# One layer of linear attention and a low-rank FFN: query-times-state product on sixteen 32x32 tiles in four banks, scores in the query's bank, four FFN value buffers

## The reference, cut to what matters

```python
xn = layernorm(x); x_norm = layernorm(xn) * ln_g + ln_b
q, k, v = split(x_norm @ W_qkv + b_qkv)
gate = sigmoid(xn @ W_gate + b_gate); gate = gate / (mean(gate) + EPS)
q = relu(q * gate) ** 2 + EPS;  k = relu(k * gate) ** 2 + EPS
# for each row t, by head:
kv = kv + k_t[:, None] * v_t[None, :];  ks = ks + k_t
out_t = (q_t @ kv) / (q_t . ks + EPS)
x1 = x + out @ W_proj + b_proj
# FFN, rank 128, hidden 2048:
y = x1 + gelu_tanh(layernorm(x1) @ U1 @ V1 + b1) @ U2 @ V2 + b2
```

## Time and profile before

| | |
|---|---|
| median of 3 runs | 1810.46 us (1809.34 to 1811.13) |
| profiled execution | 1809.73 us, span 1807.6 us |
| PE matmul busy | 1766.4 us, 98% |
| PE weight load busy | 1495.7 us, 83% |
| DVE busy | 1399.5 us, 77% |
| POOL busy | 822.7 us, 46% |
| ACT busy | 685.8 us, 38% |
| mean granted TensorE clock | 0.992 |
| DMA | 61.43 MB, mean 34 GB/s |

### The profile page before, as it was taken

One profiled execution on the slowest core, in us unless ns is written; L12 is line 12 of the kernel. 1 busy time (PEld: TensorE's weight loads), 2 busy tenths in 40 slices (PEclk: granted clock), 3 DMA queues, 4 the chain that ended last, 5 costly groups with the idle time before them and its releaser, 6 DMA issues. The chain is left out here.

```text
span 1807.6 us, 39914 instructions
## 1 busy us (share of the span) xinstructions
PE 1766.4 (98%) x16729; PEld 1495.7 (83%) x16729; DVE 1399.5 (77%) x2222; ACT 685.8 (38%) x1242; POOL 822.7 (46%) x1027
## 2 busy tenths in 40 slices
PE   7799999999999999999999999999999999999997
PEld 4688888888888888888888888888888888888876
DVE  6787787787787787777787777777777777777765
ACT  4233433433433433433433433433433433433332
POOL 3344544544544544544544544544454544454430
PEclk9899999999999999999999999999999999999999
DMA  6101010011010011010011011010100110100000
GB/s 206 34 19 36 25 36 25 24 37 36 25 36 25 25 37 33 28 36 25 25 36 29 32 29 27 30 36 25 36 25 29 32 37 24 37 24 26 30 19 24
DMA packets 34529, 61.43 MB, mean 34 GB/s; under 512 B 3672, under 2 KB 6256, under 8 KB 34352
## 3 DMA queue, kind: packets, MB, share of 16 engines
q1 hardware_dynamic: 33488, 57.31, 10.0%
q10 hardware_dynamic: 864, 1.57, 0.3%
HBM read 41.96 MB, written 16.91 MB: 33 GB/s over the span
## 5 line engine op out<-in xcount | busy, mean ns | idle before, releaser
L379 POOL TENSOR_TENSOR h_lo<-h_full,h_hi 128x512 fp32r<-128x512 f32 x244 | 313.5, 1285 | 483.5 <-DVE h_hi L605 483.5
L460 ACT ACTIVATE h_full<-ps_h,cols 128x256 f32<-128x256 f32 x512 | 211.1, 472 | 243.9 <-PE ps_h L783 236.4
L605 DVE CAST h_hi<-h_full 128x512 fp32r<-128x512 f32 x256 | 154.0, 602 | 98.2 <-ACT h_full L460 98.1
L781 PE MATMUL ps_b<-wx_hi,zt_hi 128*128 128x512 f32 x512 | 206.8, 404 | 5.0 <-DVE key_sums L711 3.1
L342 POOL TENSOR_TENSOR small<-moments,eps_col 128x1 f32<-128x1 f32 x128 | 25.7, 201 | 402.6 <-DVE moments L750 333.4
L781 PE MATMUL scores<-wx_hi,zt_hi 128*128 128x512 f32 x512 | 208.2, 407 | 0.0
L783 PE MATMUL ps_b<-wx_hi,zt_lo 128*128 128x512 f32 x512 | 204.1, 399 | 0.0
L782 PE MATMUL ps_b<-wx_lo,zt_hi 128*128 128x512 f32 x512 | 203.5, 397 | 0.0
L783 PE MATMUL scores<-wx_hi,zt_lo 128*128 128x512 f32 x512 | 202.1, 395 | 0.0
L782 PE MATMUL scores<-wx_lo,zt_hi 128*128 128x512 f32 x512 | 201.8, 394 | 0.0
L781 PE MATMUL ps_q<-h_hi,u_hi 128*128 128x256 f32 x512 | 154.1, 301 | 6.2 <-DVE h_lo L610 5.1
(11 more groups left out here) (156 smaller groups left out, 4498.6 us busy)
## 6 DMA issues: line engine op xcount, KB each, us to landing
xs<-L_attn_x SPq DMA_DIRECT2D x64, 256.0 KB, 2.7
out<-x1s SPq DMA_DIRECT2D x64, 256.0 KB, 2.1
key_sums<-carry_rows SPq DMA_DIRECT2D x60, 256.0 KB, 3.2
x1s<-L_attn_W_gate SPq DMA_DIRECT2D x4, 256.0 KB, 4.2
x1s<-L_ffn_U SPq DMA_DIRECT2D x4, 256.0 KB, 3.5
carry_rows<-key_sums SPq DMA_DIRECT2D x64, 2.0 KB
probs<-L_attn_W_qkv SPq DMA_DIRECT2D x3, 256.0 KB, 6.0
bias<-L_attn_b_qkv ACTq DMA_DIRECT2D x3, 256.0 KB, 6.8
```

The costliest lines, as they stand in the source:

```text
L379: E.tensor_tensor(h_lo[:, i % 2, :], h_full[:, i % 2, :], h_hi[:, i % 2, :].bitcast(F32), ALU.subtract).then_inc(s["h_lo_ready"], 1)
L460: last = E.activation(h_full[:, i % 2, a * GROUP:(a + 1) * GROUP], ps_h[i % 2][:, a * GROUP:(a + 1) * GROUP], ACT.Gelu_apprx_tanh, bias=b1 ...
L605: E.tensor_copy(h_hi[:, i % 2, :], h_full[:, i % 2, :]).then_inc(s["h_hi_ready"], 1)
L781: E.matmul(ps, wh, mh, start=start and i == 0, stop=False)
```

## The change

Six edits go together.

1. L944's products go to tiles (32j, 32ft), sixteen different tiles. Head group j writes bank `ps_out[j]`, partitions 32 ft. L986 accumulates there, on column tile ft. The output of a chunk now lies in 128 columns of each of four banks (`out_cols`), in another order of heads, so the rows of W_proj are loaded in that order, sixteen DMAs in place of four.
2. The product stands behind the masks: after scores, PE does `h_pair` 2, `h_pair` 3 and `q_pair` 0, then the product and L986, then tz, `q_pair` 1, L977, the sums, y, `q_pair` 2 and `q_pair` 3.
3. The eight banks are laid out anew. Scores take ps_t, ps_c, ps_d and ps_b, the query's bank, and no longer wait for `value_ready`; the product does, as ps_out is ps_c, ps_d, ps_b, ps_a.
4. `state` is double, so that the new state is written to the other half.
5. Four h buffers (`SLOTS`) in place of two.
6. ACT does gelu 2 and 3 ahead of `ot_hi`; POOL does `key_lo` ahead of the tail of pair 1; DVE takes probs ahead of the cast of pair 1, and `ot_lo` ahead of the state.

```diff
@@ -163,26 +163,33 @@
-        state = sb("state", [P, 4, KT, HEAD])
+        state = sb("state", [P, 2, 4, KT, HEAD])
         probs = sb("probs", [P, HPG, KT * P])
 ...
         qt_hi, qt_lo = pt_hi, pt_lo
-        h_hi = sb("h_hi", [P, 2, 2 * GROUP], F32R)
-        h_full, h_lo = sb_over("h_full", "h_lo", [P, 2, 2 * GROUP], F32R)
+        SLOTS = 4
+        h_hi = sb("h_hi", [P, SLOTS, 2 * GROUP], F32R)
+        h_full, h_lo = sb_over("h_full", "h_lo", [P, SLOTS, 2 * GROUP], F32R)
         lnb_wide = probs[:, 0, :].rearrange("p (k n) -> p k n", k=KT)
 ...
-        scores = ctx.enter_context(nc.psum_tensor("scores", [P, HPG * DM], F32))
-        ps_c, ps_d, ps_t, ps_a = (scores[:, j * DM:(j + 1) * DM] for j in range(HPG))
-        ps_b = bank("ps_b")
+        wide = ctx.enter_context(nc.psum_tensor("wide", [P, 5 * DM], F32))
+        ps_t, ps_c, ps_d, ps_b, ps_a = (wide[:, j * DM:(j + 1) * DM] for j in range(5))
+        scores = wide[:, 0:HPG * DM]
+        ps_scores = [ps_t, ps_c, ps_d, ps_b]
+        ps_out = [ps_c, ps_d, ps_b, ps_a]
+        out_cols = wide[:, DM:5 * DM].rearrange("p (j n) -> p j n", j=HPG)[:, :, 0:P]
         ps_h = [bank("ps_h0"), bank("ps_h1")]
         ps_q = bank("ps_q")
-        ps_scores = [ps_c, ps_d, ps_t, ps_a]
+
+        def state_of(c, turn=0):
+
+            return state[:, (c.p + c.off // 4 + turn) % 2, c.slot, :, :]
@@ -213,8 +220,8 @@
                        wx_lo[:, k, group, :], k, group) for k in range(KT)]
-        wp_v = w_proj.rearrange("(k p) n -> k p n", p=P)
-        tiles += [(wp_v[k, :, :], wp_hi[:, k, :], wp_lo[:, k, :], None, None) for k in range(KT)]
+        wp_v = w_proj.rearrange("(f j v) n -> j f v n", f=KT, j=HPG)
+        tiles += [(wp_v[k, :, :, :], wp_hi[:, k, :], wp_lo[:, k, :], None, None) for k in range(KT)]
         flat = "p k n -> p (k n)"
@@ -245,8 +252,11 @@
+        turned_tiles = range(FIRST, FIRST + KT)
+
         def tile_landed(eng, t):
-            eng.wait_ge(stage_in[stage_of(t)], 16 if t < FIRST else 16 * ((t - FIRST) // RING + 2))
+            here = [u for u in range(t + 1) if stage_of(u) == stage_of(t)]
+            eng.wait_ge(stage_in[stage_of(t)], sum(16 * KT if u in turned_tiles else 16 for u in here))
@@ -282,6 +292,11 @@
                             sp.wait_ge(s["stage_bias"], used)
+                    if t in turned_tiles:
+                        for f in range(KT):
+                            sp.dma_start(slot[f * HEAD:(f + 1) * HEAD, :], src[f, :, :])\
+                                .then_inc(stage_in[stage_of(t)], 16)
+                        continue
                     dst = slot if len(src.shape) == 2 else slot.rearrange("p (k n) -> p k n", k=src.shape[1])
@@ -376,7 +391,7 @@
                 pool.wait_ge(s["h_hi_ready"], g.done(PAIRS, i + 1))
-                E.tensor_tensor(h_lo[:, i % 2, :], h_full[:, i % 2, :], h_hi[:, i % 2, :].bitcast(F32),
+                E.tensor_tensor(h_lo[:, i % SLOTS, :], h_full[:, i % SLOTS, :], h_hi[:, i % SLOTS, :].bitcast(F32),
                                 ALU.subtract).then_inc(s["h_lo_ready"], 1)
@@ -399,12 +414,12 @@
                         h_tail(ffn, pairs[0])
-                    h_tail(ffn, pairs[1])
                 if n.exists:
 ...
                 if ffn.exists and not is_last(p):
+                    h_tail(ffn, pairs[1])
                     h_tail(ffn, pairs[2])
@@ -457,7 +472,7 @@
                 for a in range(2):
-                    last = E.activation(h_full[:, i % 2, a * GROUP:(a + 1) * GROUP],
+                    last = E.activation(h_full[:, i % SLOTS, a * GROUP:(a + 1) * GROUP],
                                         ps_h[i % 2][:, a * GROUP:(a + 1) * GROUP], ACT.Gelu_apprx_tanh,
@@ -499,13 +514,13 @@
                     gelu(ffn, pairs[2])
+                    gelu(ffn, pairs[3])
                 if c.exists:
                     act.wait_ge(s["ot_done"], c.done())
-                    E.activation(ot_hi[:, :, :].rearrange(flat), ps_b[:, :], ACT.Copy)\
+                    E.activation(ot_hi[:, :, :], out_cols, ACT.Copy)\
                         .then_inc(s["ot_hi_ready"], 1)
 ...
                 if ffn.exists:
-                    gelu(ffn, pairs[3])
                     if b % 2 == 0:
@@ -544,7 +559,7 @@
-            E.memset(state[:, :, :, :].rearrange("p b k n -> p (b k n)"), 0.0).then_inc(s["state_zero"], 1)
+            E.memset(state[:, 0, :, :, :].rearrange("p b k n -> p (b k n)"), 0.0).then_inc(s["state_zero"], 1)
             def first_stats(m):
@@ -602,12 +617,12 @@
                 dve.wait_ge(s["h_full_ready"], g.done(PAIRS, i + 1))
-                E.tensor_copy(h_hi[:, i % 2, :], h_full[:, i % 2, :]).then_inc(s["h_hi_ready"], 1)
+                E.tensor_copy(h_hi[:, i % SLOTS, :], h_full[:, i % SLOTS, :]).then_inc(s["h_hi_ready"], 1)
                 if tail:
 ...
                     dve.wait_ge(s["h_lo_ready"], g.done(PAIRS, i))
-                    E.tensor_tensor(h_lo[:, i % 2, :], h_full[:, i % 2, :], h_hi[:, i % 2, :].bitcast(F32),
+                    E.tensor_tensor(h_lo[:, i % SLOTS, :], h_full[:, i % SLOTS, :], h_hi[:, i % SLOTS, :].bitcast(F32),
                                     ALU.subtract).then_inc(s["h_lo_ready"], 1)
@@ -675,28 +690,25 @@
                     tile_tails(early_tiles)
-                if ffn.exists:
-                    if b % 2:
-                        h_head(ffn, pairs[0], finishing)
-                    h_head(ffn, pairs[1], finishing)
+                if ffn.exists and b % 2:
+                    h_head(ffn, pairs[0], finishing)
                 if c.exists:
 ...
                     E.tensor_tensor(probs[:, :, :].rearrange("p j (k t) -> p (j k) t", k=KT),
-                                    scores[:, :].rearrange("p (g t) -> p g t", g=blocks),
+                                    scores.rearrange("p (g t) -> p g t", g=blocks),
                                     causal.unsqueeze(1).broadcast_to([P, blocks, P]), ALU.mult)\
                         .then_inc(s["probs_ready"], 1)
-                    if ffn.exists:
-                        h_head(ffn, pairs[2], finishing)
+                if ffn.exists:
+                    h_head(ffn, pairs[1], finishing)
+                    h_head(ffn, pairs[2], finishing)
+                if c.exists:
+                    dve.wait_ge(s["ot_hi_ready"], c.done())
+                    E.tensor_tensor(ot_lo[:, :, :], out_cols, ot_hi[:, :, :].bitcast(F32), ALU.subtract)\
+                        .then_inc(s["ot_ready"], 1)
                     dve.wait_ge(s["state_done"], c.done())
-                    mine = state[:, c.slot, :, :].rearrange(flat)
-                    E.tensor_tensor(mine, state_cols(c), mine, ALU.add).then_inc(s["state_ready"], 1)
-                    dve.wait_ge(s["ot_hi_ready"], c.done())
-                    E.tensor_tensor(ot_lo[:, :, :].rearrange(flat), ps_b[:, :],
-                                    ot_hi[:, :, :].rearrange(flat).bitcast(F32), ALU.subtract)\
-                        .then_inc(s["ot_ready"], 1)
-                elif ffn.exists:
-                    h_head(ffn, pairs[2], finishing)
+                    E.tensor_tensor(state_of(c, 1).rearrange(flat), state_cols(c), state_of(c).rearrange(flat),
+                                    ALU.add).then_inc(s["state_ready"], 1)
                 z_tail(Chunk(p, b + 1))
@@ -836,7 +848,7 @@
                 mm = product(ps_q[:, 0:GROUP], [(u2_hi[:, 2 * i + a, :], u2_lo[:, 2 * i + a, :]) for a in range(2)],
-                             [(h_hi[:, i % 2, q], h_lo[:, i % 2, q]) for q in cols],
+                             [(h_hi[:, i % SLOTS, q], h_lo[:, i % SLOTS, q]) for q in cols],
                              start=i == 0, stop=i == PAIRS - 1)
@@ -886,12 +898,6 @@
-
-                        before = d if d.exists else Chunk(0, CHUNKS - 1)
-                        if a:
-                            pe.wait_ge(s["probs_ready"], before.done())
-                        else:
-                            pe.wait_ge(s["state_ready"], before.done())
                         product(ps[:, :], [(qt_hi[:, cols], qt_lo[:, cols])], [(v2_hi[:, :], v2_lo[:, :])])\
@@ -910,8 +916,6 @@
-
-                    pe.wait_ge(s["state_ready"], d.done())
                     if result.exists:
@@ -934,28 +938,11 @@
                         pe.wait_ge(s["den_steps"], c.done(6, 1))
-                    if not c.first:
-                        pe.wait_ge(s["state_ready"], Chunk(c.p, c.off - 4).done())
-
-                    if not c.first:
-                        for ft in range(KT):
-                            for j in range(HPG):
-                                rows = slice(HEAD * j, HEAD * (j + 1))
-                                E.matmul(ps_b[rows, ft * P:(ft + 1) * P], state[rows, c.slot, ft, :],
-                                         query_t[rows, ft, :], start=ft == 0, stop=False,
-                                         tile_position=(HEAD * j, HEAD * j), skip_group_check=True)
```

(59 more changed lines are left out.)

## The result

The changed kernel takes 1784.34 us (median of 4 runs, 1783.82 to 1784.56) against 1809.93 for the kernel before in the same comparison: ratio 0.9855, 95% interval 0.9844 to 0.9867, 25.6 us less. The forecast was 6.0 less, with 1794 as the lower end: right in sign, far too small in size. The span went from 1807.6 to 1782.3, 25.3 less.

The account below looks back on a forecast made before the run. PE's row of starts was taken to bound the kernel, with 0.3 us of waits in 58 steps. Steps +0.8, start -2.6 and end -4.2 gave -6.0 us: 1810.46 to 1804.5, range 1794 to 1814.

Parts of the forecast that it names:

- The product, 0.58: Old state product (L944) on sixteen tiles: last start at 0.38 plus drain 0.2, 0.58 us in place of 1.00.
- rival 1: Faster product: second passes fill in, 0.46 us, 7 us less over 59 steps, 1797; chance 0.20.
- The bounds (0.46 to 1.00): Product's cost: 0.46 if second passes fill in as in L977, 1.00 if tiles on the same rows take turns.
- The new wait, 3.68: PE waits for probs before the product, which starts 3.68 us after scores, latency 0.15 included: a stall of 0.25.
- The other terms of the step: After the product: probabilities times values 1.03, transposes 0.41, q_pair 1 0.89, state_cols 0.39, way back 0.10, q_pair 2 0.71.
- Outside the stretch: Outside L944 to the running sums (L1003), nothing on PE changes but q_pair 2 going behind y, counted with the stretch.
- No second stall: In each step h_lo 1 and ot_lo arrive before PE needs them, by 0.45 and 0.26 us, costing nothing.
- The start, -2.6: Steps 1 to 3: scores no longer wait for values, q_pair 0 no longer for POOL; 2.6 us less.
- The end, -4.2: Last two FFN groups, h2 and h3 ahead: 1.9 us less, twice, and 0.4 in the last chunk's step.
- Rival 2: Tiles on the same rows take turns, product stays at 1.00, 25 us more, 1829; chance 0.13, shared with a repeated stall.
- rival 3: Nothing net: the two ends don't pay because DVE's chain sets their length; 1811 us, 1809 to 1813; chance 0.15.

Follow-up runs that it names:

- experiment 4: Changed kernel with the wait for probs stated ahead of the wait for values before the product: 1781.91 us, ratio 0.9849.
- experiment 6: Changed kernel with DVE's cast of pair 1 ahead of probs again, as before the change: 1827.97 us, ratio 1.0099.
- experiment 5: Changed kernel with the scores waiting again for the values of the new chunk, as before the change: 1797.9 us, ratio 0.9939.
- the one-bank experiment: Changed kernel, product still on sixteen tiles but filling one bank after the other, column tile (j + ft) mod 4: 1785.25 us, ratio 0.9865.
- experiment 2: Changed kernel with the product's two loops exchanged, head group outermost, so successive matmuls use the same rows: 1784.39 us, ratio 0.9856.
- experiment 7: Changed kernel with PE's old order q0, h2, q1, h3 in steps without a chunk in attention (last FFN groups): 1788.66 us, ratio 0.9882.

## Why the forecast was too small

**The product, 0.58: the step that failed most.** "If starts go at that pace and the last tile's second pass still follows its first by about a round": the pace held (32 starts in 0.24), the second half did not. The last start comes 0.24 behind the first (0.51 less a mean of 0.27), not 0.38: second passes fill in, as rival 1 said with 0.46, and the product measured 0.44 to 0.45. 0.14 x 60 = 8.4 us. The bounds (0.46 to 1.00) nearly held it, but the chance on rival 1 was 0.20, on the argument that its longer passes fill in less easily than L977's, and that argument has no row behind it. The experiments on four, eight and sixteen tiles show the mechanism of the forecast (turns on tiles, 0.11 a pass) to be right: on eight tiles the starts take 0.67 less 0.27, 0.40, within the 0.33 to 0.44 that turns give. The estimate by the Trainium skill ("TensorE: Matmul & The Clock Gate", Measured speedup vs the span model), 0.38, was nearer than mine, though starts come 7.7 ns apart here and not 4.

**The new wait, 3.68.** It exists, with probs at 1.24 and PE idle in front of the product, as forecast. The latency was 0.10 to 0.11 and not 0.15, and 3.64 saves 0.04 x 59 = 2.4 us. That the first wait of the list is shorter (0.06) is shown by experiment 4.

**The other terms of the step** held to 0.02: 1.01 for 1.03 (1.2 us), 0.41, 0.89, 0.39 and 0.11 for 0.10. Together the step is 0.20 shorter, 11.8 us over 59 steps.

**Outside the stretch** "nothing on PE changes" was wrong by a little. Against the forecast the 57 steps are 12.9 + 0.8 = 13.7 shorter, 2.3 more than 0.20 x 57. These lie at the transposes of the keys: from their start to the next one is 0.39 in the steps before (947.01 to 947.40) and 0.35 after (934.70 to 935.05), and 0.04 x 57 = 2.3. Before, the keys' operation on DVE took 1.29 in the mean (1.09 after), and in the even steps x1t_lo, for which these transposes wait, ended only 0.07 ahead of them; after, 0.29 ahead. So there PE may just have been held up before the change. For the odd steps, where x1t_lo ended over 1.4 ahead, the cause is open.

**No second stall** at h_lo or ot_lo: right, with 0.23 left at ot_lo. But this cover was thin in a way that the prediction did not say: experiment 6 shows that the casts' new place is worth 43 us, and experiment 5 that the scores' new bank is worth 8.4 in steps where the kernel before never waited for values. The prediction priced neither part of the change, since nothing of the kernel before waits there.

**The start, -2.6** in waits was about right (2.3 to 2.6), and 6.8 was measured. Four steps at the steady gain of some 0.22 are 0.9. The other 3.3 or so are argued to be the clock in good part, a term that the sum had not at all: fewer waits, less time at 1.2 GHz. The row for its price is the kernel of the one-bank experiment, with the same steady steps: 0.89 in place of 1.00 between 60 and 90 us, 6.6 us at the lower level, and from the scores of step 1 to those of step 3 it is 1.6 us longer. (The kernel of experiment 2 has 0.94 there and is 0.4 longer.) Between 50 and 120 us the kernel before has some 10 us more at the lower level than the changed one; an estimate by these two prices is 1.2 to 2.4 us. No run changes the clock alone, so the cause of these 3.3 us isn't shown. No wait in either list is for the loads of W_proj, which the prediction put at 0.

**The end, -4.2:** 3.8 of it from the order of the last groups, for which experiment 7 measured 4.3. 5.7 came off: the waits of q pairs fell by 4.9, those for zs by 0.8, for queries by 0.5, and 0.4 for h_full came new. The last three the sum had not.

Rival 2 is refuted by experiment 2 and the product's 0.44; rival 3 by both ends, which did pay. The time fell below the range because errors of one sign added up, while the lower end covered little more than the first: over the 57 steps the product 8.0, the latency 2.3, the keys' transposes 2.3 and the other terms 1.1, then the start 4.2 and the end 1.5. The double state, the four h buffers and the new orders of ACT and POOL were not taken back one by one. The terms above add up to what was measured in the steady part, so all that they can do there is to keep a wait from coming up, and how much that is worth is not shown.

## What to carry to other kernels

In this kernel small fp32 matmuls on PE cost starts plus one drain as long as each tile is used by one product only; count how often a tile comes back, not banks or rows. When an operation is moved from in front of another, look for what it had been covering there: here values in every even step and the casts beside POOL. Where a step is bound by a chain (scores, probs, product, ot_lo), put fillers behind the link and not in front of it, and state the wait that comes last first.

## What was not expected of the hardware

- A second use of the sixteen tiles costs 0.55, more than the first use with its drain (0.44).
- A wait stated first before a matmul releases it 0.06 behind the other engine's end, one stated second 0.11: 2.4 us in this kernel.
- A DVE operation of 0.43 took 1.35 beside a POOL operation that had started 0.22 earlier, and one that took 1.09 in the changed kernel took 1.80. A shift of some tenths of a us in a step's phase decides which operations meet: 16 us between two kernels with the same work.
- The granted clock at the start differed between kernels with the same work (1.00 and 0.89 from 60 to 90 us), with a start that was 1 to 2 us longer.
